# Self attention in two halves of eight heads: the maximum, the shift, the exponential and the scores each in two instructions, the residual behind the shift, and the rotations written out with constant waits

## The reference

```python
x = x + scan(norm(x))               # 16 dependent steps of a small learned map
x = x + x0(norm(x), context)        # cross attention, 16 heads of 8, 77 keys, a mask
x = x + experts0(norm(x))           # 8 experts, the best 2 weighted
x = x + s1(norm(x))                 # self attention, 16 heads of 8, 128 keys, ALiBi bias
x = x + x1(norm(x), context)        # cross attention again
x = x + experts1(norm(x))
```

```python
energy = einsum('nqhd,nkhd->nhqk', q, k) + alibi_bias(s, s)
attn = softmax(energy / sqrt(HEAD_DIM), axis=-1)
out = einsum('nhqk,nkhd->nqhd', attn, v).reshape(n, s, 128) @ Wo.T + bo
```

## Time and profile before

| what | value |
|---|---|
| time, median of 3 runs | 977.45 us (976.96 to 977.49) |
| the profiled execution: its time, its span | 976.2 us, 974.4 us |
| busy share of the span: PE, DVE, ACT, POOL | 86%, 71%, 58%, 22% |
| self attention `s1`, from its first to its last VectorE instruction | 492.37 to 650.79 us |
| cross attention `x0`, first and last maximum | 171.64 and 264.68 us |
| cross attention `x1`, first and last maximum | 658.46 and 744.67 us |

### The profile page before, as it was taken

How to read it: one execution, slowest core, us unless ns; L and a number is a source line. 1 busy time by engine, 2 the same in 40 slices (tenths; PEclk the granted TensorE clock), 3 DMA queues, 4 the chain that set the end, 5 groups by cost and what they waited for, 6 DMA issues and landing times. The chain is left out here.

```text
span 974.4 us, 20356 instructions
## 1 busy us (share of the span) xinstructions
PE 837.2 (86%) x6519; PEld 633.2 (65%) x6534; DVE 688.3 (71%) x1509; ACT 565.1 (58%) x1085; POOL 213.5 (22%) x414
## 2 busy tenths in 40 slices
PE   4889997777769999999948888857777799999997
PEld 2666664555558888888725565545555688888885
DVE  6544443699967777777756778748997677777776
ACT  3532222566628777777705555535665487777774
POOL 5210001766620000000043322216663200000000
PEclk9975555799968999999959999988999699999999
DMA  7100000111000000000000000001110000000000
GB/s 175 4 1 0 0 0 22 44 45 43 23 1 1 1 1 1 0 0 0 1 0 2 1 0 0 1 22 52 48 43 12 1 1 0 12 0 11 0 11 11
DMA packets 33763, 14.44 MB, mean 15 GB/s; under 512 B 15550, under 2 KB 31407, under 8 KB 33711
## 3 DMA queue, kind: packets, MB, share of 16 engines
q1 hardware_dynamic: 33711, 13.79, 5.6%
HBM read 12.70 MB, written 1.05 MB: 14 GB/s over the span
## 5 line engine op out<-in xcount | busy, mean ns | idle before, releaser
L1400 DVE TENSOR_TENSOR f_h_lo<-f_h,f_h_hi 128x512 fp32r<-128x512 f32 x256 | 177.0, 692 | 99.4 <-ACT f_h_hi L1385 97.8
L1382 ACT ACTIVATE f_h<-f_p_h,b 128x512 f32<-128x512 f32 x256 | 179.3, 700 | 83.6 <-PE f_p_h L1339 80.8
L1385 ACT ACTIVATE f_h_hi<-f_p_h,b 128x512 fp32r<-128x512 f32 x256 | 180.2, 704 | 0.0
L1337 PE MATMUL f_p_h<-f_xT_hi,w_hi 128*128 (+1 forms) x256 | 108.7, 424 | 1.8 <-PEq L1222 1.7
L1350 PE MATMUL f_p_yT<-f_h_hi,w_hi 128*128 128x512 f32 x256 | 102.2, 399 | 1.1 <-DVE f_h_lo L1400 1.0
L1338 PE MATMUL f_p_h<-f_xT_lo,w_hi 128*128 (+1 forms) x256 | 102.1, 399 | 0.0
L1339 PE MATMUL f_p_h<-f_xT_hi,w_lo 128*128 (+1 forms) x256 | 102.0, 398 | 0.0
L1352 PE MATMUL f_p_yT<-f_h_hi,w_lo 128*128 128x512 f32 x256 | 101.1, 395 | 0.0
L1351 PE MATMUL f_p_yT<-f_h_lo,w_hi 128*128 128x512 f32 x256 | 100.4, 392 | 0.0
L1466 DVE SCALAR_TENSOR_TENSOR x<-f_p_y,f_wts,x 128x128 f32 (+1 forms) x256 | 72.1, 344 | 6.1 <-PE f_p_y L1361 5.4
L881 POOL TENSOR_SCALAR s_var<-s_mv 128x1 f32<-128x1 f32 x16 | 3.6, 223 | 285.6 <-DVE s_mv L952 285.6
(11 more groups left out here) (229 smaller groups left out, 1711.2 us busy)
## 6 DMA issues: line engine op xcount, KB each, us to landing
x_w_raw<-in_w SPq DMA_DIRECT2D x32, 256.0 KB, 2.7
x<-in_x SPq DMA_DIRECT2D x4, 256.0 KB, 4.2
out<-x SPq DMA_DIRECT2D x4, 256.0 KB, 2.3
c<-in_ctx SPq DMA_DIRECT2D x1, 616.0 KB
ctxT<-in_ctxT SPq DMA_DIRECT2D x1, 616.0 KB
sq<-in_squares SPq DMA_DIRECT2D x1, 576.0 KB
alibi<-in_alibi SPq DMA_DIRECT2D x1, 512.0 KB, 3.6
sq<-in_squares SPq DMA_DIRECT2D x1, 256.0 KB, 3.5
```

The costliest lines, as they stand in the source:

```text
L1337: mm(p_h[:, k, :], w_hi[:, 2 * e, of], x_hi, start=True, stop=False)
L1382: nc.scalar.activation(h[:, k % 2, :], p_h[:, k, :], ACT.Relu, bias=b1[:, e, k:k + 1]).then_inc(h_sb, 1)
L1385: nc.scalar.activation(h_hi[:, e % 2, k, :], p_h[:, k, :], ACT.Relu, bias=b1[:, e, k:k + 1]).then_inc(h_hi_ready, 1)
L1400: nc.vector.tensor_tensor(h_lo[:, e % 2, k, :], h[:, k % 2, :], h_hi[:, e % 2, k, :], ALU.subtract).then_inc(h_lo_ready, 1)
```

## The change

It has four parts.

1. `staggered` no longer makes a loop: all 21 steps of all three attentions are written out with constant waits, and all calls of `pass_waits` in the attentions go.
2. In `s1`, the maximum, the shift and the exponential each become two instructions over eight heads (1024 numbers of a row each); the other attentions keep theirs, as `group_sets` has one entry there. `scored`, `top_done`, `shifted` and `exped` count halves.
3. TensorE scores `s1` in two halves, each released by the matching half of the shift of the batch before; `turn_p` waits for its own half of the exponential.
4. In VectorE's list of `s1` the maximum stands first, then `scale_out`, the shift, the residual, and `count` and `normalise` last. GpSimd's and ScalarE's lists keep their order.

```diff
-def staggered(eng, stages, first=6):
...
+def staggered(stages):
 
     lags = [lag for lag, _ in stages]
-    last = NB + min(min(lags), 0) // 2 * 2
...
+    for k in range(min(lags), NB + max(lags)):
         for lag, stage in stages:
             if 0 <= k - lag < NB:
                 stage(k - lag, (k - lag) % 2)
-    for k in range(min(lags), first):
-        peeled(k)
-    with eng.Fori(0, (last - first) // 2) as i:
-        for u in range(2):
-            for lag, stage in stages:
-                stage(i * 2 + (first + u - lag), (first + u - lag) % 2)
-    for k in range(last, NB + max(lags)):
-        peeled(k)
...
+        group_sets = [slice(0, NG // 2), slice(NG // 2, NG)] if own else [slice(0, NG)]
+        pieces = [(of, part) for of in group_sets for part in parts]
...
                 def masked_k(b, p):
 
                     if own:
                         pool.wait_ge(k_flat_sb, b + 1)
-                    wait(pool, scored, b - 1)
-                    pass_waits(pool, m)
+                    wait(pool, scored, len(group_sets) * (b - 1))
...
                     s.done(nc.vector.bn_stats(stats[:, p, :], at(x, b)))
-                    pass_waits(dve, m)
                     s.done(nc.vector.bn_aggr(mv[:, p, :], stats[:, p, :]))
...
                 def find_top(b, p):
-                    dve.wait_ge(scored, b + 1)
-                    nc.vector.tensor_reduce(top[:, :].rearrange("p (g h) -> p g h", h=HG), scores, AX.X, ALU.max).then_inc(top_done, 1)
+                    for n, of in enumerate(group_sets):
+                        dve.wait_ge(scored, len(group_sets) * b + n + 1)
+                        nc.vector.tensor_reduce(tops[:, of, :], scores[:, of, :, :], AX.X, ALU.max).then_inc(top_done, 1)
 
                 def shift(b, p):
 
-                    dve.wait_ge(top_done, b + 1)
                     wait(dve, p_turned, NS * (b - 1))
...
-                    for part in parts:
+                    for n, (of, part) in enumerate(pieces):
                         k0, k1 = part[2:]
...
+                        dve.wait_ge(top_done, len(group_sets) * b + min(n + 1, len(group_sets)))
+                        nc.vector.tensor_tensor(prob_of(p, part).rearrange("p (g h) k -> p g h k", h=HG)[:, of, :, :], scores[:, of, :, k0:k1],
+                                                tops[:, of, :].unsqueeze(3).to_broadcast([P, of.stop - of.start, HG, k1 - k0]),
+                                                ALU.subtract).then_inc(shifted, 1)
...
                 if own:
-                    staggered(dve, [(4, scale_out), (-1, count),
-                                    (4, residual), (2, find_top), (2, shift), (-1, normalise)])
+                    staggered([(2, find_top), (4, scale_out), (2, shift), (4, residual), (-1, count), (-1, normalise)])
...
                 def exps(b, p):
-                    for n, part in enumerate(parts):
-                        act.wait_ge(shifted, len(parts) * b + n + 1)
-                        nc.scalar.activation(prob_of(p, part), prob_of(p, part), ACT.Exp, scale=exp_scale).then_inc(exped, 1)
+                    for n, (of, part) in enumerate(pieces):
+                        act.wait_ge(shifted, len(pieces) * b + n + 1)
+                        to = prob_of(p, part)[:, HG * of.start:HG * of.stop, :]
+                        nc.scalar.activation(to, to, ACT.Exp, scale=exp_scale).then_inc(exped, 1)
...
                 def score(groups):
                     def run(b, p):
+                        if own:
+                            wait(pe, shifted, len(pieces) * (b - 1) + groups[-1] // 2 + 1)
+                        else:
+                            wait(pe, shifted, len(pieces) * b)
                         if groups[0] == 0:
                             pe.wait_ge(q_sb, b + 1)
                             pe.wait_ge(k_sb, b + 1)
-                            wait(pe, shifted, len(parts) * b)
...
-                        if groups[-1] == NG - 1:
-                            last.then_inc(scored, 1)
+                        last.then_inc(scored, 1)
...
-                        pe.wait_ge(exped, len(parts) * (b + 1))
                         for g in groups:
+                            pe.wait_ge(exped, len(pieces) * b + (1 + g // 2 if own else len(pieces)))
...
                 if own:
-                    staggered(pe, [(2, score(range(NG))), (3, turn_p((0, 1))), (4, project_o),
+                    staggered([(2, score((0, 1))), (2, score((2, 3))), (3, turn_p((0, 1))), (4, project_o),
                                    (3, turn_p((2,))), (0, turn_in), (3, turn_p((3,))), (0, project), (3, mix)])
```

More of the change, by code:

```diff
@@ L828, in attention @@
         p_o = ctx.enter_context(nc.psum_tensor(f"{name}_p_o", [P, 512], F32))
+        tops = top[:, :].rearrange("p (g h) -> p g h", h=HG)
         scores = p_s[:, :, 0:GW].rearrange("p g (h k) -> p g h k", k=T)
@@ L938, in add_bias @@
                         pool.wait_ge(normed, b + 1)
-                        pass_waits(pool, m)
                         nc.gpsimd.tensor_tensor(at(x, b), at(x, b), m[f"bo_{name}"][:, :], ALU.add).then_inc(biased, 1)
-                staggered(pool, [(-1, rstd_of), (0, add_bias), (0, copy_mask), (L, masked_k), (0, set_zero),
+                staggered([(-1, rstd_of), (0, add_bias), (0, copy_mask), (L, masked_k), (0, set_zero),
                                  (L + 1, copy_v), (0, weights_lo)])
@@ L992, in _ @@
                 if own:
-                    staggered(dve, [(4, scale_out), (-1, count),
-                                    (4, residual), (2, find_top), (2, shift), (-1, normalise)])
+                    staggered([(2, find_top), (4, scale_out), (2, shift), (4, residual), (-1, count), (-1, normalise)])
                 else:
-                    staggered(dve, [(3, scale_out), (-1, count), (1, find_top), (3, residual), (1, shift), (-1, normalise)])
+                    staggered([(3, scale_out), (-1, count), (1, find_top), (3, residual), (1, shift), (-1, normalise)])
             @block.scalar
@@ L1017, in copy_q @@
                     act.wait_ge(projected, b + 1)
-                    wait(act, scored, b - 1)
+                    wait(act, scored, len(group_sets) * (b - 1))
                     if name == "x1":
@@ L1045, in _ @@
                 if own:
-                    staggered(act, [(1, copy_kv), (1, copy_q), (3, copy_pT((0, 1))), (3, copy_pT((2,))), (0, turn_in), (3, copy_pT((3,))), (2, exps)])
+                    staggered([(1, copy_kv), (1, copy_q), (3, copy_pT((0, 1))), (3, copy_pT((2,))), (0, turn_in), (3, copy_pT((3,))), (2, exps)])
                 else:
-                    staggered(act, [(2, copy_pT((0, 1))), (0, weights_hi), (0, turn_in), (2, copy_pT((2,))),
+                    staggered([(2, copy_pT((0, 1))), (0, weights_hi), (0, turn_in), (2, copy_pT((2,))),
                                     (0, copy_q), (1, exps)])
@@ L1135, in _ @@
                 if own:
-                    staggered(pe, [(2, score(range(NG))), (3, turn_p((0, 1))), (4, project_o),
+                    staggered([(2, score((0, 1))), (2, score((2, 3))), (3, turn_p((0, 1))), (4, project_o),
                                    (3, turn_p((2,))), (0, turn_in), (3, turn_p((3,))), (0, project), (3, mix)])
                 else:
-                    staggered(pe, [(1, score(range(NG))), (2, turn_p((0, 1))), (3, project_o), (0, turn_in),
+                    staggered([(1, score(range(NG))), (2, turn_p((0, 1))), (3, project_o), (0, turn_in),
                                    (2, turn_p((2,))), (0, project), (2, mix)])
```

6 lines of the change are left out of this document (removed).

## The result

The changed kernel takes 1012.46 us (median of 4 runs, 1008.9 to 1014.41) against 977.47 for the kernel before (976.96 to 978.6): 1.0352 times as long, with an interval of 1.0322 to 1.0383. It is slower, as forecast, but above the range. The profiled execution took 1012.03 us, with a span of 1009.3.

A forecast was written before the change was run, and what follows sets the result against it. It took a chain of waits through shift, exponential, `project_o` and residual to set `s1`'s step. The profiled 976.2 + 23.1 (`s1`) - 5.5 (`x0`, `x1`) = 993.8; the median is 1.25 above, so 995 us, range 984 to 1007.

The forecast's parts named there:

- which ring closes: In `s1`, a new chain of maximum, shift, `count`, GpSimd, scores, next maximum sets the step: 10.3 us against 8.55.
- Half of the scores: Term of the `s1` step: two bias matmuls about 0.49 plus products 0.71 on TensorE, 1.20 us.
- 13 steps with `count`: In `s1`, steps from the first to the fourteenth maximum, at 10.3 us each.
- TensorE is slower, which I let cancel: First two `s1` steps: no `scale_out` (1.19 less) but slower TensorE, taken to cancel.
- The last two steps: End of `s1`, without `count`: TensorE's order makes a ring through `project_o`, transposes, `mix` and scores, 9.5 us each.
- Draining is taken as equal: End of `s1`: draining was counted as no difference between the kernels.
- no increments, constant waits: `x0` and `x1`: increments gone, 0.22 us in about 12 steps of each, -5.3; register waits a little; -5.5 taken.
- (1 is refuted): Rival: increments not the gaps' cause; step 10.5, `s1` +26, `x0` and `x1` give nothing; 1003 us; 15%.
- (2): Rival: halves overlap as meant and VectorE alone sets the `s1` step, 7.8 us; kernel faster, 959 us; 7%.
- (3): Rival: TensorE's own ring, 9.5 us a step, sets all steps of `s1`; 985 us; 14%.
- (4): Rival: TensorE doesn't hold its clock in `s1`; step about 14 us, total 1040 us; 4%.
- (5): Rival: gain and loss cancel within 0.2%, needing steps of 9.0 to 9.2 us; 4%.

The follow-up runs named there:

- e1: The changed kernel with `count` moved to the head of VectorE's list in `s1`; 1003.76 us, ratio 1.0263.
- e2: The changed kernel with `masked_k` first in GpSimd's list of `s1`, VectorE's list as changed; 990.91 us, ratio 1.013.
- e4: The kernel before with steps written out with constant waits and without the `pass_waits` increments, old order, one piece; 968.16 us, ratio 0.9911.
- e8: The kernel before with its steps written out with constant waits, all `pass_waits` increments kept; 973.05 us, ratio 0.9944.
- e3: The changed kernel with all scores in one piece again, signals behind the second and fourth product, other halves kept; 1012.26 us, ratio 1.0341.
- e6: e4 with the change's VectorE list for `s1` and no halves; 1013.23 us, ratio 1.0356.
- e9: e4 with VectorE's `s1` list as `scale_out`, `count`, maximum, residual, shift, `normalise`, nothing halved; 957.18 us, ratio 0.9792.
- e7: The changed kernel with VectorE's `s1` list as `scale_out`, `count`, maximum, residual, shift, `normalise`, and scores whole, other halves kept; 957.18 us, ratio 0.9784.
- e10: e7 with the scores also in two halves, as in the change; 977.4 us, ratio 0.9994.

## Why the prediction was wrong, step by step

**Right: which ring closes.** The step was forecast as maximum, shift, `count`, GpSimd, scores, next maximum, with VectorE's wait near 2.5 us (measured 2.76). e1 opens it on VectorE, e2 on GpSimd; both bring the step from 11.12 to 10.30.

**Wrong: the size of one term, "Half of the scores".** It took "the first four records of products" as 0.71 us, as if they were the products of two groups. Two groups take 1.13. The same trace of before has the whole group of eight, and its second four:

```profile
556.29 1.14 PE L1097 MATMUL s_p_s<-s_kT,s_qT 32*128 32x512 f32 x8
...
556.82 0.61 PE L1097 MATMUL s_p_s<-s_kT,s_qT 32*128 32x512 f32 x4
```

and the changed kernel's four come as two and two:

```profile
580.97 0.70 PE L1084 MATMUL s_p_s<-s_kT,s_qT 32*128 32x512 f32 x2
...
581.50 0.59 PE L1084 MATMUL s_p_s<-s_kT,s_qT 32*128 32x512 f32 x2
```

Four records start together where four groups are scored, two where two are, and the next as many start 0.53 later in both. So the row's four were one record of each of the four groups, and the products of half of the groups take both rounds too. The error enters the ring twice:

| part of the ring, us | forecast | measured |
|---|---|---|
| first to second half of the maximum | 1.15 | 1.60 (of it 0.37 waiting for the second half of the scores) |
| second half of the maximum to the reciprocal | 1.15 | 1.14 |
| reciprocal; product | 0.98; 0.21 | 0.98; 0.21 |
| both halves of the shift | 2.30 | 2.26 |
| residual; statistics to aggregation | 0.21; 0.31 | 0.20; 0.32 |
| aggregation to the weights of the scores | 2.67 | 2.69 |
| weights to the next maximum | 1.31 | 1.72 |
| step | 10.3 | 11.12 |

Two terms are off, by 0.45 and 0.41; all others are within 0.04. In VectorE's timeline the first halves of the maximum of the first, the fourteenth and the last batch are these:

```profile
502.79 1.22 DVE L948 TENSOR_REDUCE s_top<-s_p_s 128x8 f32<-128x1024 f32 x1 [4.13 <-PE s_p_s L1084]
...
648.87 1.23 DVE L948 TENSOR_REDUCE s_top<-s_p_s 128x8 f32<-128x1024 f32 x1 [2.76 <-PE s_p_s L1084]
...
670.78 1.23 DVE L948 TENSOR_REDUCE s_top<-s_p_s 128x8 f32<-128x1024 f32 x1 [5.14 <-PE s_p_s L1084]
```

- *13 steps with `count`*: forecast 133.9, measured 648.87 - 502.79 = 146.08, an error of 12.2. Eleven are 11.12 each, 9.0 over the forecast. The first two take 12.47 and 11.28, at a granted clock of 0.58 from 500 to 526 us; "TensorE is slower, which I let cancel" left out 3.1 more.
- *The last two steps*: forecast 9.5 each, measured 10.30 and 11.61, together 2.9 too little. 10.30 is the same step as in e1 and e2, so TensorE's ring was mis-sized by the same term (9.5 + 0.45 + 0.41 = 10.4). In the last step `mix` fell into the window of 664 to 668 above, at a granted clock of 0.67, and took 3.45 us (665.69 to 669.14) where it took 1.96 in the step before.
- *The first maximum*: 13.33 us after the stage's start against 14.84, 1.5 sooner (forecast 1.6).
- *"Draining is taken as equal"*: 16.56 against 15.72, 0.8 short.

The errors add up to 12.2 + 2.9 + 0.8 + 0.1 = 16.0, which is `s1`'s 39.14 - 23.1. The range was too narrow for the same reason: it allowed 0.3 us of error in a step, and half of the products was never set against the whole, 1.14 us, which would have given 10.3 + 2 x 0.43 = 11.2.

**Right: no increments, constant waits.** -5.65 in `x0` and `x1` against -5.5, with the gap at 0.04 and cross steps 0.2 shorter. e4 and e8 show the increments as the cause of the gaps and of 0.21 a step. That the sum came so close owes something to luck: from e8 to e4, where only the increments go, `x0` and `x1` fall from 212.12 to 209.04 us, 3.1 and not 5.3, and the rest came from `x0` without its loop (107.99 in e8 against 110.53). The gain from the loop and its register waits, 4.4 to 5.5 us over the whole kernel, was costed at "a little".

**The rivals.** The increments were the gaps' cause (1 is refuted). VectorE never came to set the step (2). TensorE's ring is there, 0.8 behind (3), and decides in e1, e2 and the last two steps. The clock held within the steady steps of the changed kernel (4), though not in all of e1, e3 and e6. Gain and loss didn't cancel (5). Whether halves could pay in an order where ScalarE, not TensorE, is last was not tried.

## What to carry to other kernels

When a stage moves on one engine, ask for every engine that waits for it what stands behind that wait in its own queue: here two VectorE instructions of together 0.5 us held GpSimd's mask multiply, and with it the scores, and one line of order made 45 us (e4 to e6). To fill a wait, move into it the one thing that was waited for and leave the early producer where it is (e9, 957.2). Don't split products that stand on row strips beside each other along those strips: here half cost as much as all.

## What was unexpected of the hardware

- Two groups' products on two row strips take 1.13 us, four groups' on four strips 1.14. With TensorE busy for 94% of the time, halving by strips cost 20.2 us (e7 to e10).
- One semaphore increment between VectorE's wait for its statistics and the aggregation costs 0.11 us (0.15 against 0.04), and all of them together 3 to 5 us (e4 against e8).
- In `x0` of e8 the same `normalise`, started 0.13 us before the same instruction of GpSimd, took 1.49 us in most steps and 0.34 in three, which made these steps 5.1 to 5.6 us long instead of 6.21.
- The granted clock fell in single steps of the slow orders (0.86 in e6, 0.85 in e3, 0.67 at the end of the changed kernel). It stayed at 1.00 from 520 to 610 us with steps of 7.7 and 8.9 (e9, e10), but also from 526 to 660 with steps of 11.12 (the changed kernel), so a long step alone doesn't bring a dip. TensorE was busy for 7.42 of the 11 us before one in e6, and for 101.5 of 134 us in the changed kernel. What triggers a dip is open.
